# The mean of x by a matmul that is already there, a DRAM row and an accumulating DMA, with low-rank fetch and V/H order moved

## What is computed

```python
x = L0_attn_X                                   # [16, 2048, 1024] float32, two sequences per core
q, k, v = x @ Wq.T + bq, x @ Wk.T + bk, x @ Wv.T + bv
scores = q @ k.T / sqrt(1024), masked where j > i
attn = softmax(scores, axis=-2)                 # over i, so each key j has its own normaliser
x = layernorm(x + attn @ v)                     # no gamma, no beta
h = x
for blk in range(3):                            # six dequantised 1024x1024 weights with low-rank parts
    y = gelu(layernorm(qlora(h, 2*blk)))
    h = qlora(y, 2*blk + 1) + h
x = layernorm(x + h)
```

## Time and profile before

| | |
|---|---|
| median of 3 runs | 1446.7 us (1445.36 to 1462.48) |
| the profiled execution | 1443.28 us |
| its span on core 5, the slowest | 1441.7 us (the cores: 1429.3 to 1441.7) |
| busy: PE / DVE / ACT / POOL | 1339.1 / 698.4 / 750.5 / 424.5 us |
| mean granted clock of TensorE | 0.965 to 0.972 |
| DMA | 192.17 MB, 133 GB/s on the mean |

### The profile page before, as it was taken

One profiled execution on the slowest core, in us unless ns is written; L12 is line 12 of the kernel. 1 busy time (PEld: TensorE's weight loads), 2 busy tenths in 40 slices (PEclk: granted clock), 3 DMA queues, 4 the chain that ended last, 5 costly groups with the idle time before them and its releaser, 6 DMA issues.

```text
span 1441.7 us, 21149 instructions; the slowest of 8 cores (1429.3 to 1441.7 us)
## 1 busy us (share of the span) xinstructions
PE 1339.1 (93%) x6724; PEld 620.1 (43%) x6724; DVE 698.4 (48%) x1474; ACT 750.5 (52%) x1104; POOL 424.5 (29%) x308
## 2 busy tenths in 40 slices
PE   6979999969899999888999999999989999999994
PEld 2434444434344444443444444445534444444552
DVE  1225555433344354416464365468634624736774
ACT  0135226653213356422784686576668748847741
POOL 4022353786623256654000019100100000650010
PEclk9988999989999999989999999999999999999998
DMA  9956545686855343485011035215641010550022
GB/s 137 217 164 201 172 146 139 198 239 204 282 177 203 117 147 131 167 292 224 11 59 46 14 104 169 78 32 190 222 143 58 2 59 1 182 169 1 30 103 103
DMA packets 70699, 192.17 MB, mean 133 GB/s; under 512 B 5696, under 2 KB 16192, under 8 KB 67520
## 3 DMA queue, kind: packets, MB, share of 16 engines
q1 hardware_dynamic: 48192, 133.40, 28.5%
q0 software_dynamic: 22400, 57.42, 14.3%
HBM read 158.03 MB, written 46.14 MB: 142 GB/s over the span
## 4 chain that ended last, share of the span: by engine, by line
PE 79%; DVE 5%; POOL 5%; issue 4%; ACT 3%; DMA 2%; another core or an unknown queue 1%; DVEq 0%; SPq 0%; ACTq 0%; POOLq 0%
PE ps L212 79%; ACT POOLT L216 3%; DVE POOLT L220 2%; POOL POOLT L612 2%; POOL POOLT L652 2%; DMA POOLT<-wq 1%; POOL POOLT L102 1%; DVE SM L994 1%; DMA POOLT<-bv_h 1%; DVE SM L229 1%; DVE POOLT L226 0%; POOL POOLT L394 0%; DVEq L108 0%; DVE POOLT L721 0%
## 5 line engine op out<-in xcount | busy, mean ns | idle before, releaser
L212 PE MATMUL ps<-POOLT 128*128 128x512 bf16 (+2 forms) x5600 | 1262.0, 378 | 30.7 <-DMA POOLT<-lb_h 8.7
L212 PEld LDWEIGHTS ps<-POOLT 128*128 128x128 bf16 (+1 forms) x5600 | 540.2, 99 | 685.1 <-issue 113.0
L216 ACT ACTIVATE POOLT<-ps,SM 128x512 bf16<-128x512 f32 (+4 forms) x396 | 262.6, 683 | 258.7 <-PE ps L212 156.5
L220 DVE TENSOR_TENSOR POOLT<-POOLT 128x512 bf16<-128x512 bf16 (+1 forms) x448 | 254.4, 604 | 211.9 <-ACT POOLT L216 191.6
L216 ACT ACTIVATE POOLT<-POOLT 128x512 bf16<-128x512 f32 (+4 forms) x234 | 175.8, 762 | 228.0 <-DMA POOLT<-qw_t 83.6
L220 DVE TENSOR_TENSOR POOLT<-ps,POOLT 128x512 bf16<-128x512 f32 (+1 forms) x176 | 117.0, 688 | 177.0 <-PE ps L212 151.9
L952 POOL TENSOR_TENSOR POOLT<-POOLT 128x512 f32<-128x512 f32 x64 | 89.6, 1424 | 373.8 <-DMA POOLT<-x1s 366.2
L394 POOL TENSOR_TENSOR POOLT<-POOLT 128x1024 f32<-128x1024 f32 x48 | 112.7, 2348 | 275.2 <-DMA POOLT<-sc_t 131.5
L216 ACT ACTIVATE POOLT<-POOLT,CF 128x512 bf16<-128x512 bf16 x192 | 154.3, 808 | 26.4 <-DVE POOLT L220 25.6
L212 PE MATMUL ps<-POOLT,CB 128*128 128x512 bf16 x320 | 116.5, 394 | 47.6 <-ACT POOLT L216 38.3
L216 ACT ACTIVATE POOLT<-POOLT,SM 128x512 bf16<-128x512 f32 (+2 forms) x120 | 110.0, 918 | 78.3 <-DVE SM L223 43.1
(11 more groups left out here) (53 smaller groups left out, 303.8 us busy)
## 6 DMA issues: line engine op xcount, KB each, us to landing
POOLT<-qw_t SPq DMA_DIRECT2D x48, 512.0 KB, 4.2
POOLT<-sc_t SPq DMA_DIRECT2D x48, 512.0 KB, 5.5
POOLT<-weffs SPq DMA_DIRECT2D x24, 1024.0 KB, 7.8
POOLT<-xt SPq DMA_DIRECT2D x16, 1024.0 KB, 10.6
x1s<-POOLT POOLq DMA_DIRECT2D x16, 1024.0 KB, 5.4
POOLT<-x1s SPq DMA_DIRECT2D x8, 2048.0 KB, 10.9
POOLT<-x1s SPq DMA_DIRECT2D x64, 256.0 KB, 3.2
out<-POOLT POOLq DMA_DIRECT2D x28, 512.0 KB, 4.1
```

Source lines behind the costliest of these rows:

```text
L212: return pe.put(lambda e: e.matmul(out, lhsT, rhs, start=start, stop=stop), *after, sig=sig)
L216: return act.put(lambda e: e.activation(out, in_, func, bias=bias, scale=scale, accum_out=acc), *after)
L220: return dve.put(lambda e: e.tensor_tensor(out, a, b, op), *after)
```

## The change

- `c_bias` uses a two-column weight: the second column is -1/1024 in each block, so the second row of each result is minus the mean of x. The loops are exchanged: chunk is now the inner loop, so that successive matmuls write to partitions 0, 32, 64 and 96 in turn. The four ACT copies come after all 32 matmuls. The four mean rows (2 KB each) are stored to a DRAM tensor `means` by a DMA on SP.
- `mean_x`, its matmuls, ACT copy and POOL subtractions are gone. `centre_r` puts two DMAs on POOL's queue instead, each of which adds the mean row (one row read for all 128 partitions and four blocks) to a 1 MB group of fp32 x in place.
- `centre_r` of chunk 0 follows `c_bias` or V, that of chunk 1 is put out 6 groups later, that of chunk 2 six groups after the end of `pv_chunk` 1, that of chunk 3 ahead of `pv_chunk` 3. `load_r` of chunk 3 comes two groups earlier, `var_mm` comes 5 groups later in chunks 2 and 3 instead of 3.
- The low-rank factors are fetched between the second and the third bf16 chunk of x.
- In sequence 1, H of chunk n+1 now comes ahead of V of chunk n.
- `c_bias` counts 20 units in place of 36, and the 8 units of each `mean_x` are gone, so the dequantisation steps fall later against the rest.

```diff
-    def dma(self, slot, out, in_, *after):
+    def dma(self, slot, out, in_, *after, **how):
...
-        k_x = [load_x(0, ic, ic) for ic in range(4)]
+        k_x = [load_x(0, ic, ic) for ic in range(2)]
+        load_lora(0, 4)
+        k_x += [load_x(0, ic, ic) for ic in range(2, 4)]
...
-        k_w = dve.put(lambda e: e.tensor_copy(hl[:, 32:40], sm[:, S_W:S_W + 8]), t1)
+        hw = hl[:, 32:48].rearrange("p (c t) -> p c t", t=2)
+        k_w = v_ts1(hw[:, :, 1], cf[:, C_ONE:C_ONE + 8], -1.0, ALU.mult, k_cf)
+        k_w = v_ts1(hw[:, :, 0], sm[:, S_W:S_W + 8], 1.0, ALU.mult, t1)
...
         def c_bias(seq, slots):
             b, fr = bank_take()
             b2, fr2 = bank_take()
             ts = []
+            for c in range(EC):
+                for jc in range(4):
+                    g = 32 * jc
+                    p = mm(ps[b][g:g + 2, :], hl[:, 32 + 2 * c:34 + 2 * c], XT[slots[jc]][c],
+                           c == 0, c == EC - 1, k_w, k_x[jc], *fr, sig=c == EC - 1)
             for jc in range(4):
                 g = 32 * jc
-                for c in range(EC):
-                    p = mm(ps[b][g:g + 1, :], hl[:, 32 + c:33 + c], XT[slots[jc]][c],
-                           c == 0, c == EC - 1, k_w, k_x[jc], *fr, sig=c == EC - 1)
-                ts.append(a_act(mu[g:g + 1, :], ps[b][g:g + 1, :], AF.Copy, p, *mu_free))
+                ts.append(a_act(mu[g:g + 2, :], ps[b][g:g + 2, :], AF.Copy, p, *mu_free))
             bank_give(b, ts[-1])
+            k_mean[0] = sp.dma(s_mean, means[seq], plf[1:98:32, A_MU:A_MU + 512], ts[-1])
...
-            mu_free[:] = [p]
+            mu_free[:] = [p, k_mean[0]]
...
-            units[0] += 36
+            units[0] += 20
...
-        def mean_x(seq, ic, xs):
...
+        def centre_r(seq, ic):
+
+            row = bass.AP(means, (seq * 4 + ic) * TT, [[0, 128], [0, 4], [1, TT]])
+            for h, g in enumerate(x_groups(4 * seq + ic)):
+                k_xm[(seq, ic, h)] = pool.dma(
+                    s_ra[g], RG[g].rearrange("p (c t) -> p c t", t=TT), row,
+                    k_rl[(seq, ic, h)], k_mean[0], accum_op=ALU.add)
...
-                t = v_tt(r, ps[b][:], r, ALU.add, p, k_xm[(seq, ic, et // 2)])
+                t = v_tt(r, ps[b][:], r, ALU.add, p, k_xm[(seq, ic, et // 4)])
...
-                after_groups(3, lambda c=et, q=q, ta=ta: var_mm(c, q, ta))
+                after_groups(3 if ic < 2 else 5, lambda c=et, q=q, ta=ta: var_mm(c, q, ta))
...
-                if (ic, et) in ((1, 7), (2, 5)):
+                if (ic, et) in ((1, 7), (2, 3)):
                     while pieces:
                         pieces.pop(0)()
                     load_r(seq, ic + 1)
-                if et == 7 and ic < 3:
-                    after_groups(1 if ic == 0 else 3, lambda: pieces.extend(
-                        [lambda: sub_piece((seq, ic + 1))] * 4))
+                    if ic == 1:
+                        after_groups(6, lambda: centre_r(seq, 2))
...
+                    else:
+                        v_chunk(seq, ic - 1, sl[ic - 1])
                     if ic == 2:
                         while pieces:
                             pieces.pop(0)()
                         load_r(1, 1)
-                    v_chunk(seq, ic, sl[ic])
+                v_chunk(seq, 3, sl[3])
                 c_bias(seq, sl)
...
-            mean_x(seq, 0, sl[0])
-            for _ in range(4):
-                pieces.append(lambda k=(seq, 0): sub_piece(k))
+            centre_r(seq, 0)
+            after_groups(6, lambda: centre_r(seq, 1))
...
-                    if seq == 0 and jt in (3, 7, 11):
+                    if seq == 0 and jt % 4 == 3:
                         k_x_next[jt // 4] = load_x(1, jt // 4, jt // 4, xt_read[jt // 4])
                 if ic == 2:
                     z_row(prev)
-                while subs[(seq, ic)]:
-                    sub_piece((seq, ic))
-                if ic + 1 < 4:
-                    mean_x(seq, ic + 1, sl[ic + 1])
-                    if seq == 0 and ic == 2:
-                        k_x_next[3] = load_x(1, 3, 3, xt_read[3])
+                if ic == 3:
+                    centre_r(seq, 3)
                 pv_chunk(seq, ic)
```

More of the change, by code:

```diff
@@ L97, in put @@
         return (self.sem, self.n)
-    def dma(self, slot, out, in_, *after):
+    def dma(self, slot, out, in_, *after, **how):
         todo = self._waits(after)
         slot.n += 16
-        self.items.append((todo, lambda e: e.dma_start(out=out, in_=in_), slot.sem, 16))
+        self.items.append((todo, lambda e: e.dma_start(out=out, in_=in_, **how), slot.sem, 16))
         return (slot.sem, slot.n)
@@ L139, in build_program @@
     out_h = nc.dram_tensor("out", [NSEQ, T, E], F32, kind="ExternalOutput").ap()
+    means = nc.dram_tensor("means", [NSEQ, 4, TT], F32)
     x1s = nc.dram_tensor("x1s", [NSEQ, 4, 128, EC * TT], F32)
@@ L257, in load_x, with load_lora @@
             return pool.dma(s_x[s], XT3[s], xsrc[seq][:, :, ic * TT:(ic + 1) * TT], *after)
-        k_x = [load_x(0, ic, ic) for ic in range(4)]
+        s_lora = slot()
+        lora_free = [None]
+        k_lora = [None]
+        def load_lora(first, n):
+            la = plb[:, 2 * A_LORA:2 * A_LORA + 1024]
+            lb = plb[:, 2 * A_LORA + 1024:2 * A_LORA + 2048]
+            pool.dma(s_lora, la[0:32 * n], la_h[first:first + n].rearrange("w r e -> (w r) e"),
+                     lora_free[0])
+            k_lora[0] = pool.dma(s_lora, lb[0:32 * n],
+                                 lb_h[first:first + n].rearrange("w r e -> (w r) e"),
+                                 lora_free[0])
+        k_x = [load_x(0, ic, ic) for ic in range(2)]
+        load_lora(0, 4)
+        k_x += [load_x(0, ic, ic) for ic in range(2, 4)]
         k_wv = [sp.dma(slot(), f32v(A_V + o * 1024, 1024), wv_t[o * 128:(o + 1) * 128, :],
@@ L262, in build_program @@
         k_bv = sp.dma(s_bv, f32v(A_BVC, 1024), bv_h, k_x[1])
-        s_lora = slot()
         k_eps = dve.put(lambda e: e.memset(col(S_EPS), EPS))
@@ L367, in build_program @@
         dq_ab = [None, None]
-        lora_free = [None]
-        k_lora = [None]
         k_weff = {}
[L372 to L379, removed]
         def dq_load(k):
@@ L436, in dq_slot @@
                 dq_load(n + 1)
-        load_lora(0, 4)
         Hb = b16v(A_H, 16384).rearrange("p (j c t) -> p j c t", c=EC, t=128)
@@ L469, in build_program @@
         mu_free = []
+        k_mean = [None]
+        s_mean = slot()
+        s_ra = [slot() for _ in range(4)]
         rs_free = []
```

## The result

The changed kernel takes 1564.3 us (1558.4 to 1566.7) against 1445.4: **ratio 1.081, 95% interval 1.077 to 1.085**. It is 8% slower where 2% faster was forecast. The profiled execution has a span of 1563.0 us on core 2.

The account below looks back on a forecast made before the run. PE's matmuls plus its waits, chiefly 35.0 us for ACT in attention, were taken as the bound. Terms 11.6 + 6.5 + 8.9 - 0.2 - 8 + 5.5 + 2.6 + 3.6 + 0.2 = 30.7 us off 1446.7 gave 1416.0; eight in ten within 1394 to 1450.

Parts of the forecast that it names:

- price of an accumulating DMA: Mean added to x on POOL's DMA queue: 8 us of queue time per MB, range 4.4 to 17.
- slow rival: Accumulations share one 2 KB row and read and write back their destination: 17 us per MB, 1486 us; chance 0.14.
- the clock: Lower granted clock after PE's stalls: some 5.5 us back where stalls vanish, none in chunk 2 of sequence 0.
- Chunk 2 of sequence 0: PE's stall in `pv_chunk` 2: about 12 us should remain near 300; term -0.2 us, ends +12.7 and -9.
- chunk 3 there: `pv_chunk` 3 of sequence 0, without a stall before: a new stall of 7 us, waiting for ACT's square.
- sequence 1: PE's stalls there: chunk 2's goes entirely, 8.9 us saved; chunk 3 costs 1 us.
- Low-rank factors: PE's 8.68 us wait at the start falls to about 5 and becomes ACT's: 3.6 us saved.
- V/H order: PE's 4.00 us wait near V's bias row stays; only the kind of eviction changes: 0.2 us saved.
- `c_bias`: Constant stage: 32 matmuls take 2.5 us instead of 4.42, ACT copies exposed 0.6; 1.3 us saved twice, 2.6 us.
- POOL's DMA queue would take POOL's place: Rival: at 11 to 13 us per MB, sequence 0's DMA chain gives most back: 1425 to 1450 us; chance 0.17.

## Why the prediction was wrong

**The price of an accumulating DMA** is the step that failed. I took 8 us of queue time per MB, from plain stores and casting loads, with 17 as the upper end. In the changed kernel the first burst of four lands at 212.6, 231.0, 244.0 and 260.9 us: 16.1 us apart on the mean, and 22.0 to 60.1 from the issues. With distinct rows the same four land at 199.6, 208.1, 216.5 and 224.2, 8.2 us apart. So 8 us was the price of an accumulation of distinct rows; one row read for all doubled it, and nothing in the trace before had a shared row. For the slow rival I named both the shared row and the read and write back of the destination, and priced neither; the runs show that the shared row does nearly all of it. The page's share of POOL's queue points the same way: estimated from it, (0.214 x 1420.4 - 0.143 x 1441.7) / 16 = 6.1 us of all engines' time per accumulation with distinct rows, and 10.7 with the shared one.

**What such a price costs** was mis-stated too. 16.1 us is close to the 17 of the slow rival, for which I worked out 1486 us (its terms add up to -40.1, not -39); it came to 1564. Three things were missing. I had looked at the dequantisation only through POOL's waiting, and not through its stores in the same DMA queue: that these gate DVE through their buffers cost some 32 us (the run with them on SP). The stalls sit where I looked, but larger: chunk 3's of 24.52 and 7.38, chunk 2's of 25.79 and 15.30, and 20.23 us at the head of the second stage behind the last accumulation. And the clock, where I had 5.5 us back and 1.5 in the slow case, took some 16 us more instead (1278.4 - 1262.0). SP's loads come late with the accumulations. The Trainium skill, "DMA: Bandwidth & Descriptors", section "Issuing engines are not separate DMA queues", says that all issuers' DMAs interleave on the same sixteen engines; the trace agrees, with SP's 512 KB loads at 15.5 us to landing beside the accumulations where it was 4.1.

**With the price mended** the forecast's working holds: the one run with distinct rows took 1422.1 us and the kernel with four adjacent copies 1424.8, against 1416.0. PE's timeline of the latter:

```profile
309.39 0.58 PE L213 MATMUL ps<-POOLT,CB 128*128 128x512 bf16 x1 [16.06 <-ACT POOLT L217]
346.72 0.59 PE L213 MATMUL ps<-POOLT,CB 128*128 128x512 bf16 x1 [9.01 <-ACT POOLT L217]
...
597.96 0.41 PE L213 MATMUL ps<-POOLT,CB 128*128 128x512 bf16 x1 [2.05 <-ACT POOLT L217]
626.45 0.38 PE L213 MATMUL ps<-POOLT,CB 128*128 128x512 bf16 x1 [2.44 <-ACT POOLT L217]
```

Chunk 2 of sequence 0: about 12 us forecast, 16.06 measured; chunk 3 there: 7, measured 9.01; sequence 1: none and 1, measured 2.05 and 2.44. The chain casting load, accumulation, store, load that I drew for sequence 0 is thus borne out in its places, not tested link by link. The accumulations land in 14.8 us in the middle.

**The small terms.** Low-rank factors: 3.6 us forecast, 1445.8 x 0.0044 = 6.4 us measured (2.9 to 10.0), the wait 3.71 us for ACT as described. V/H order: 0.2 forecast, none measured, releaser as described. `c_bias`: 2.6 us forecast, none measured (between 2.5 gained and 3.6 lost); the 32 matmuls take 1.90 us where I took 2.5. In like rows that is 4.49 / 1.90 = 2.4 times. The Trainium skill, "TensorE: Matmul & The Clock Gate", section "Measured speedup vs the span model", has 2.38 times for three column tiles, and this trace agrees, with four; 4.42 / 2.38 is an estimate of 1.9 us, not the 2.3 that I wrote. The term failed behind the matmuls: PE stands 1.36 us for ACT's copy, and the low clock comes earlier and takes the rest of the gain back.

**The rivals.** That POOL's DMA queue would take POOL's place was right in kind, and the slow case had 0.14 of the chance. Of its two reasons one was the cause. What I lacked was a row for a shared source; with none, the range had to reach further than the busy cast load.

**Open.** Whether the limit on a shared row is in one DRAM bank, in the path to it, or in what the eight cores ask at once is not told by these runs. Nor is it told why packets of 8 KB take the price of sharing away.

## What to carry to other kernels

Don't let a large DMA read one short row for every partition: here it cost the other queues their time as well, and four adjacent copies of the row, read in packets of 8 KB, mended it. Few copies are enough: 128 of them held SP's queue up and came out 56 us slower than four. Before a transfer is put into a queue, list what stands behind it and who waits for that, buffers that are freed by a store included. If a row is only to be added under a matmul's result, one more matmul in the same PSUM group does it with no queue at all.

## What the runs showed of the hardware

- An accumulating POOL-queue DMA of 1 MB whose 512 packets all read one 2 KB row took 32.0 us to landing in the middle; with 128 packets on each of four rows 18.9; with 128 packets of 8 KB over four adjacent rows 14.8. A plain one from the one row, in 256 packets, took 28.5.
- An accumulating DMA of distinct 2 KB rows took 13.1 us in the middle and 8.7 at the quickest; four in a burst landed 8.2 us apart, and 16.1 with the shared row.
- Reading one row of SBUF 128 times into DRAM, 256 KB, took 25.2 us to landing with four such in flight, and held SP up to 9.6 us at the issue.
- 32 matmuls of two columns by 512 that take the four column quarters in turn took 1.90 us, as did those of one column; eight after another in the same quarter had made it 4.49.
